# Scan loop of a selective state space layer: skip products, read-out of the sums, and gate at other states

## What is computed

```python
h = x * rsqrt(mean(x * x) + eps) * norm_w
u, res = split(h @ in_w, 2)
u = silu(conv(u) + conv_b)
dt, Bm, Cm = split(u @ x_proj_w, [64, 80])
delta = softplus(dt @ dt_w + dt_b)
dA = exp(delta * A)                      # A = -exp(A_log), one per channel and state
dBu = (delta * u) * Bm
s = dA_t * s + dBu_t                     # step over the 2048 positions
y_t = sum over the 16 states of s * C_t
y = (y + u * D) * silu(res)
return y @ out_w + x
```

## Time and profile before

| | |
|---|---|
| median of 3 runs | 3350.98 us (3346.10 to 3351.53) |
| the profiled execution | 3348.16 us, span 3346.4 us |
| busy, share of the span | PE 3190.6 us (95%), DVE 2794.2 (84%), ACT 2504.1 (75%), POOL 2438.6 (73%) |
| scan loop in that execution | first drive 1583.1 us, end of the last read-out 1812.7 us |
| gate_out L1639 | 8 of 128x512, median 686 ns |
| L1703 (POOL, in the stacks) | 192 of 128x1024, mean 1947 ns |

### The profile page before, as it was taken

How to read it: one execution, slowest core, us unless ns; L and a number is a source line. 1 busy time by engine, 2 the same in 40 slices (tenths; PEclk the granted TensorE clock), 3 DMA queues, 4 the chain that set the end, 5 groups by cost and what they waited for, 6 DMA issues and landing times.

```text
span 3346.4 us, 120438 instructions
## 1 busy us (share of the span) xinstructions
PE 3190.6 (95%) x51618; PEld 2522.9 (75%) x51618; DVE 2794.2 (84%) x3204; ACT 2504.1 (75%) x3163; POOL 2438.6 (73%) x1233
## 2 busy tenths in 40 slices
PE   7999999999999999998888899999999999999999
PEld 5888888887887887874333788888888878788777
DVE  7888888888888888877897888888888888888886
ACT  5777777777777777777675677777777777777776
POOL 6777777777776776763898777777768768768764
PEclk8999999999999999999999999999999999999999
DMA  3333333233233332221000332323323323323322
GB/s 113 89 76 87 75 83 88 68 90 85 67 89 84 73 83 65 71 72 60 1 0 0 86 76 69 93 68 83 91 65 88 88 69 86 91 71 80 74 64 69
DMA packets 142299, 245.22 MB, mean 73 GB/s; under 512 B 32397, under 2 KB 34638, under 8 KB 141774
## 3 DMA queue, kind: packets, MB, share of 16 engines
q1 hardware_dynamic: 141774, 237.51, 27.9%
HBM read 35.01 MB, written 1.05 MB: 11 GB/s over the span
## 4 chain that ended last, share of the span: by engine, by line
PE 39%; issue 4%; DVE 3%; POOL 2%; ACT 2%; DVEq 0%; POOLq 0%; ACTq 0%
PE PS L270 7%; PE PS L390 6%; PE PS L214 4%; PE PS L410 4%; PE PS L216 3%; PE PS L215 3%; PE PS L331 3%; PE PS L527 2%; ACT ARENA L912 1%; DVE ARENA L1619 1%; PE PS L474 1%; PE PS L475 1%; PE PS L476 1%; POOL ARENA L1806 1%; PE PS L433 1%
## 5 line engine op out<-in xcount | busy, mean ns | idle before, releaser
L1695 POOL TENSOR_TENSOR ARENA<-ARENA,RN 128x1024 f32<-128x1024 f32 x192 | 365.4, 1903 | 456.5 <-ACT RN L902 456.5
L270 PE MATMUL PS<-C,ARENA 128*128 128x128 f32 x4608 | 613.5, 276 | 34.4 <-ACT ARENA L912 16.3
L1687 POOL TENSOR_TENSOR ARENA<-ARENA 128x1024 f32<-128x1024 f32 x192 | 468.4, 2439 | 233.9 <-DVE ARENA L1284 233.0
L270 PEld LDWEIGHTS PS<-C,ARENA 128*128 128x128 f32 x4608 | 512.0, 141 | 111.0 <-issue 76.6
L214 PE MATMUL PS<-WL,XH 128*128 128x512 f32 x1152 | 490.0, 425 | 14.0 <-DVE ARENA L1284 7.5
L965 ACT ACTIVATE ARENA<-PS 64x1024 f32<-64x1024 f32 x384 | 390.2, 1016 | 98.0 <-PE PS L270 94.7
L1681 POOL TENSOR_TENSOR ARENA<-ARENA 128x1024 f32<-128x1024 f32 x192 | 458.0, 2385 | 6.5 <-DVE ARENA L1269 6.4
L216 PE MATMUL PS<-WH,XH 128*128 128x512 f32 x1152 | 455.3, 395 | 0.0
L215 PE MATMUL PS<-WH,XL 128*128 128x512 f32 x1152 | 453.4, 394 | 0.0
L390 PE MATMUL PS<-ARENA 128*64 128x64 f32 x12288 | 401.1, 224 | 40.7 <-DVE ARENA L1322 24.5
L390 PEld LDWEIGHTS PS<-ARENA 128*64 128x64 f32 x12288 | 376.1, 138 | 75.8 <-issue 75.8
(11 more groups left out here) (155 smaller groups left out, 6493.9 us busy)
## 6 DMA issues: line engine op xcount, KB each, us to landing
ARENA<-ARENA SPq DMA_DIRECT2D x1152, 128.0 KB, 2.4
ARENA<-ARENA SPq DMA_DIRECT2D x768, 64.0 KB, 2.1
ARENA<-in_wqkv SPq DMA_DIRECT2D x36, 512.0 KB, 4.9
ARENA<-in_wo SPq DMA_DIRECT2D x12, 512.0 KB, 3.9
ARENA<-in_w SPq DMA_DIRECT2D x12, 341.0 KB, 4.0
ARENA<-in_w SPq DMA_DIRECT2D x12, 192.0 KB, 3.9
X<-in_xT SPq DMA_DIRECT2D x4, 256.0 KB, 5.0
out<-X SPq DMA_DIRECT2D x1, 768.0 KB, 3.5
```

The source lines that it names most:

```text
L270: last = nc.tensor.transpose(PS[:, slot, 128 * j:128 * j + 128], src[:, 128 * j:128 * j + 128], ident)
L1687: nc.gpsimd.tensor_tensor(KN[n % 2], KN[n % 2], T2, ALU.add).then_inc(k_add, 1)
```

## The change

The first accumulation of a chunk starts the sum itself (`start=n == 0`), and the two skip products stand behind the eighth state's accumulation (n == 7), ahead of `mamba_out` in PE's order. In turn k % 16 == 1 ACT copies the finished sums of the chunk before out of banks 6 and 7 into Y (two copies of 128x512), and the next chunk's first accumulation waits for these (m_yc). DVE's gate is one product Y * RES of 128x1024 in SBUF, between the scans of state k % 16 == 4, and raises m_yg. `mamba_out` stands at k % 16 == 9 and its copy by ACT at 10. The last chunk's gate (`gate_last`) reads PSUM in two products as before. The rest of the lines renames semaphores.

```diff
 # accumulate(pe, k)
             pe.wait_ge(m_pr, k + 1)
             if k == 0:
                 pe.wait_ge(m_dl, 4)
-                pe.wait_ge(m_dg, 1)
             elif n == 0:
-                pe.wait_ge(m_yd, 2 * h)
+                pe.wait_ge(m_yc, 2 * h)
             for b in range(2):
-                if n == 0:
-                    nc.tensor.matmul(PSB[:, 6 + b, :], DG[:, 128 * b:128 * b + 128], UC[:, h, b, :], start=True, stop=False,
-                                     skip_group_check=True)
-                last = nc.tensor.matmul(PSB[:, 6 + b, :], ident, PR[k % 2][:, b, :], start=False, stop=n == 15,
+                last = nc.tensor.matmul(PSB[:, 6 + b, :], ident, PR[k % 2][:, b, :], start=n == 0, stop=n == 15,
                                         skip_group_check=True)
             last.then_inc(m_y, 1)
+            if n == 7:
+                pe.wait_ge(m_dg, 1)
+                for b in range(2):
+                    nc.tensor.matmul(PSB[:, 6 + b, :], DG[:, 128 * b:128 * b + 128], UC[:, h, b, :], start=False, stop=False,
+                                     skip_group_check=True)
 # tensor_mamba
-                if 0 <= h < 3 and k % 16 == 5:
+                if 0 <= h < 3 and k % 16 == 9:
                     pe.wait_ge(m_bev, k + 1)
                     mamba_out(pe, h, 2 * (k % 2))
 # mamba_out(pe, c, bank)
-            pe.wait_ge(m_yd, 2 * c + 2)
+            pe.wait_ge(m_yg, c + 1)
 # scalar_mamba
+            def keep_sums(h):
+                act.wait_ge(m_y, 16 * h + 16)
+                for b in range(2):
+                    act.activation(Y[:, h, b, :], PSB[:, 6 + b, :], ACT.Copy).then_inc(m_yc, 1)
...
-                if k > 16 and k % 16 == 6:
+                if k > 16 and k % 16 == 10:
                     h = k // 16 - 1
                     act.wait_ge(m_out, h + 1)
                     act.activation(X[:, chunks[h]], PSB[:, 2, :], ACT.Copy).then_inc(m_done, 1)
...
                     evacuate(k + 1)
+                if k > 1 and k % 16 == 1:
+                    keep_sums(k // 16 - 1)
 # vector_mamba
-                if h >= 0 and k % 16 == 1:
-                    gate_out(dve, h)
+                if h >= 0 and k % 16 == 4:
+                    dve.wait_ge(m_yc, 2 * h + 2)
+                    nc.vector.tensor_tensor(Y[:, h, :, :], Y[:, h, :, :], RES[:, h, :, :], ALU.mult).then_inc(m_yg, 1)
                 scan(k, 1)
-        def gate_out(dve, h):
-            dve.wait_ge(m_y, 16 * h + 16)
+        def gate_last(dve):
+            dve.wait_ge(m_y, 64)
             for b in range(2):
-                nc.vector.tensor_tensor(Y[:, h, b, :], PSB[:, 6 + b, :], RES[:, h, b, :], ALU.mult).then_inc(m_yd, 1)
+                last = nc.vector.tensor_tensor(Y[:, 3, b, :], PSB[:, 6 + b, :], RES[:, 3, b, :], ALU.mult)
+            last.then_inc(m_yg, 1)
```

More of the change, by code:

```diff
@@ L175, in build @@
             "dt", "min", "ex", "sp", "dl", "du"))
-        m_bc, m_bev, m_cs, m_pr, m_dg, m_y, m_yd, m_out, m_done = (sem("m_" + n) for n in (
-            "bc", "bev", "cs", "pr", "dg", "y", "yd", "out", "done"))
+        m_bc, m_bev, m_cs, m_pr, m_dg, m_y, m_yc, m_yg, m_out, m_done = (sem("m_" + n) for n in (
+            "bc", "bev", "cs", "pr", "dg", "y", "yc", "yg", "out", "done"))
         m_da, m_db, m_sc = ([sem(f"m_{n}{b}") for b in range(2)] for n in ("da", "db", "sc"))
@@ L227, in q_project @@
                     if r == 1:
-                        pe.wait_ge(m_yd, 8)
+                        pe.wait_ge(m_yg, 4)
                         mamba_out(pe, 3, 7)
@@ L1434, in vector_stack @@
             if r == 1:
-                gate_out(dve, 3)
+                gate_last(dve)
             nc.vector.memset(B[64:128, 0:1], 0.0).then_inc(edge_set, 1)
@@ L1728, in pool_stack @@
             if r == 1:
-                pool.wait_ge(m_yd, 8)
+                pool.wait_ge(m_yg, 4)
                 pool.wait_ge(m_out, 3)
```

## The result

The changed kernel took 3360.57 us (median of 8 runs, 3358.16 to 3362.32), the one before 3350.71 us (8 runs, 3344.45 to 3351.74): ratio 1.0034 (that of the means, 3360.40 and 3349.14), 95% interval 1.0025 to 1.0043. By the medians it is 9.9 us slower. That is just inside the wide range (3344 to 3361), but above the sum's own range (up to 3357) and beyond the 0.2% within which I forecast no change, with a chance of 0.66; slower had 0.28. The sign of the sum was right, its size (+4.3) was less than half.

A forecast was written before the change was run, and what follows sets the result against it. POOL was taken to bound the scan loop, with DVE close behind. The terms -4.0 - 2.1 + 5.2 + 7.2 - 2.0 gave +4.3 us on 3348.2, so 3352.5 us; own range 3348 to 3357, wide range 3344 to 3361.

The forecast's parts named there:

- part 4: Gate as one 128x1024 SBUF product at n = 4 contends with POOL: +7.2 us, between 5.9 and 9.8.
- cheap gate: Gate product getting in behind POOL's running instruction, costing POOL 1.97 us; assumed for two of three gates.
- dear: Gate product waiting until POOL's read-out and next drive are over, costing POOL 3.25 us; assumed for one gate.
- Part 1: Gate leaves the chunk's second state, so POOL's 1.32 us wait goes three times: -4.0 us, bounds -4.0 to 0.
- Part 2: Skip products leave the first accumulation at the loop's start, shortening POOL's 2.78 us wait: -2.1 us, between -2.8 and -1.5.
- Part 3: Skip products behind the eighth state's accumulation lengthen the chain through mamba_out by 1.72 us, three times: +5.2 us, bounds 0 to 5.2.
- Part 5: Input product of state 24 hidden in DVE's wait before the double drive of state 27: -2.0 us, bounds -2.0 and 0.
- The rival Clock: Low clock from the gap at state 20 until state 24 slows PE's chain: 6.3 us a chunk, 3371; chance 0.08.
- gates all at the dear price: Slower rival: 3.77 us a gate and nothing hidden at state 24, sum +10.4, 3358.6 us; chance 0.15.

The follow-up runs named there:

- old gate: Changed kernel with the gate again in two products from PSUM at n = 1, no ACT copies: 3348.49 us (kernel before beside it 3349.98), loop 230.16.
- no gate: Changed kernel without the multiplication by silu(res) in chunks 0 to 2, ACT's copies releasing mamba_out: 3349.89 us, loop 226.22.
- gate with the clock filled: Changed kernel with PE issuing the spread of states 23, 39 and 55 four times: 3355.28 us, loop 235.90.
- second execution: The changed kernel profiled once more, with no edit: 3355.58 us, loop 237.68.

## Why the prediction was right or wrong

The sum gave +4.3 us and the profiled loop +12.4. Two steps of the prediction failed. The larger: the sum had no term for a low clock behind the gates, which took 5.5 us of that loop (1.8 us in each of three chunks). The smaller: part 4 took the cheap gate to be the commoner case, and all three were dear, 2.5 us more. The other parts held, one of them partly by luck.

The loop's 12.4 us split by the chain of kernels: before to old gate +0.7, to no gate -3.9, to gate with the clock filled +9.7, to the changed kernel +5.9.

- **Part 1** (-4.0) is right: -3.94. In the changed kernel ACT's copies end in time and no 1.32 us is left.
- **Part 2** (-2.1) holds only where the clock rises early. With the old gate it did (small waits of 0.53 and 0.41 us in place of 2.78: -1.84; with the 0.52 before read-out 14, which is gone too, it is most of the 2.45 by which chunk 0 is shorter). In the changed kernel's profile the waits up to the seventh read-out add up to 2.65 us: nothing gained there. The step that failed took PE's two products away and let the clock rise when it had risen before. Yet chunk 0 as a whole is 1.9 us shorter, since the input product of state 8 took 2.67 us there and not 3.70, and the 0.52 before read-out 14 is gone; that the total came out near the forecast is luck in the changed kernel. The two go together in all fourteen traces: where the clock rose 8.7 to 11.8 us after POOL's first drive (six) that product took 3.69 to 3.72 us, where it rose after 14.3 to 15.3 (eight) it took 2.66 to 2.68. The changed start has both kinds, so the edit alone did not make the clock rise late.
- **Part 3** (+5.2) is right: +1.75 a chunk for 1.72. The 4.84 in the changed kernel is this 4.44 and 0.40 from the late PE.
- **Part 5** (-2.0) is right: chunk 1 changed by -0.33 with the old gate, where parts 3 and 5 gave -0.25. Parts 2, 3 and 5 together gave +1.1, measured +0.7.
- **Part 4** (+7.2) is the step that failed on the gate. "Getting in is the commoner case; I take two gates at 1.97 and one at 3.25": 18 of 18 gates that stood between the scans of state 20, 36 or 52 in six runs took 3.62 to 3.66 us. The price of such a gate was right (3.25 forecast, 3.2 measured), its frequency was not; three at that price are 9.7, in the range I gave (5.9 to 9.8). Two rows of L1562 are too few for odds, and they differ between executions: of the 28 input products in the fourteen traces, 15 got in, 10 were passed over (3.63 to 3.72 us) and three came as POOL's read-out was ending (1.20).
- **The rival Clock**, at 0.08, came true at a smaller size, and is the larger of the failed steps. I judged it by the low stretch behind state 8, over some 10 us behind a scan, and asked whether it would reach the end of read-out 23 at full length. It did not have to: reaching the accumulation of state 37, which began 12 us behind the gate's scan (1728.85) and for which read-out 39 waits, it made PE 0.75 us late, held two drives by 0.16 and 0.23 us and left 0.4 in the stall: with smaller gaps 1.8 us a chunk, not 6.3. I had put nothing for it in the sum.
- The case "gates all at the dear price" had the gate right, but not that nothing is hidden at state 24.

With three dear gates (9.7 for 7.2, +2.5) and the low clock (1.80 + 1.85 + 1.86 = 5.5) the sum would have been 4.3 + 2.5 + 5.5 = 12.3, which is the profiled loop's +12.4; with the low clock in one chunk of three, as in the second execution, 8.6, where the loop gave +8.2 on the first profile of before. The median of +9.9 lies between them. How often the low stretch stands in the eight runs is not shown by profiles; their granted clock over the whole span was 0.986 to 0.989, nearer to the first profile (0.988) than to the second (0.991).

**Who is served at the shared port stays open.** The Trainium skill ("SBUF — State Buffer", section "SBUF: two separate sides") says that the instruction that starts first holds the port for its whole length. The rows agree that the two take turns: a product that waited ends 1.08 us after POOL's instruction, nearly the 1.20 that it takes alone, and a POOL drive behind a product that got in takes about 2.28 us in place of 1.3. The Trainium skill does not say who comes next, and the rule I weighed in part 4 (the waiting one is served) fails in all 21 gates of the seven runs: POOL's next instruction went past the waiting product, in three of them twice. Of the input products of the same form 15 did get in, at 1.89 to 2.68 us, and 10 did not. Neither asking earlier nor a later release of the drive changed it.

One ordering that no run tested sorts the rows: for how long POOL's read-out had been running when the product was asked for. In the fourteen traces 43 products between two scans were asked for during a read-out. The 13 asked for 0.78 to 0.98 us after its start got in, the 28 at 0.99 to 1.22 did not (all 18 gates lie there, at 1.05 to 1.19), and two at 1.29 and 1.56 did again. This was read from the rows afterwards, and why there should be such a stretch is not known. No run moved the gate out of it; none varied DVE's own instruction ahead of the product, or the place of the operands in SBUF. So what decides is not shown.

## What to carry to other kernels

A VectorE product with both inputs in SBUF, put beside a GpSimd stream that never pauses, should be priced at the rest of the running GpSimd instruction plus the whole of the next one, unless rows of that very place show the cheaper case: here 3.6 us for 1.2 us of work, paid by 28 of 43 such products. So reading one input from PSUM was cheaper even at the price of a wait of 1.3 us. Before moving such a product, try its other side of the neighbouring instruction: behind both scans the PSUM gate cost 0.5 us. And a stall of one engine also idles TensorE, so add what follows if its clock falls, as a cost of its own.

## What the hardware showed that I had not expected

- A waiting VectorE product was passed over by POOL twice in a row: asked for at 1712.79, 0.08 us ahead of a read-out of 2.45 us and a drive, done after 4.83 us.
- Whether and how long the granted clock falls behind the same rest of PE varies between executions of one program: not at all, 3 or 10 us, and 0 or 1.8 us of the loop in a chunk. At the loop's start it rose 2.8 to 5.9 us after PE's first accumulation began in six executions (1589.14 to 1594.0 before, 1589.78 to 1594.6 with the old gate), and 8.5 to 9.5 us after it in eight (1590.51 to 1600.0 in the changed kernel).
- The price of a contended product can be the same to 0.04 us in 18 cases, and yet differ by 1 us between executions for the input product at state 8, in step with the time at which the clock had risen, 14 to 19 us earlier.
